# A vision tower on one core: another order in attention, slot 0's passes split around the logits, and other slots for VectorE's high parts

## The reference

```
h = tok(x); h = concat(cls, h)                         # 64 x 170 x 128
h = h + attn(layernorm(h))    # a graph convolution: relu, two adjacency products, a projection
h = h + ffn(layernorm(h)):
    hx = layernorm(x, g, b); q, k, v = hx@Wq, hx@Wk, hx@Wv       # 2 heads of 64
    q, k = l2norm(q)*sqrt(64)*qn_g, l2norm(k)*sqrt(64)*kn_g
    y = (softmax(causal(q k^T / 8)) v) @ Wo
    gate = softmax(y @ gate_W + gate_b)                # 8 experts
    hid = gelu(y @ W1[e] + b1[e])                      # 128 -> 512 for each e
    out = sum_e gate[e] * (hid @ W2[e] + b2[e])        # 512 -> 128
```

## Time and profile before

| | us |
|---|---|
| three runs | 1540.8, 1546.08, 1545.88 |
| median | 1545.88 |
| profiled execution | 1542.88 |
| its span, first to last instruction | 1540.7 |
| TensorE busy in the span | 1462.2 (95%) |
| VectorE, ScalarE, GpSimd busy | 1238.6, 1082.8, 329.9 |

### The profile page before, as it was taken

The page is one execution under the profiler, slowest core; times in us unless marked ns, Lnnn a source line. Parts: engine busy times, 40 slices in busy tenths (PEclk is TensorE's granted clock), DMA queues, the critical chain, the costliest instruction groups (busy, mean ns, idle before and its releaser), DMA issues.

```text
span 1540.7 us, 31400 instructions
## 1 busy us (share of the span) xinstructions
PE 1462.2 (95%) x10991; PEld 994.6 (65%) x10991; DVE 1238.6 (80%) x2585; ACT 1082.8 (70%) x1861; POOL 329.9 (21%) x337
## 2 busy tenths in 40 slices
PE   7898889999999999999999999999999999999998
PEld 4554556666666666666666666666666666666665
DVE  6768798878888888888888788888788888887765
ACT  5232667777777777786777777786777777777766
POOL 1135044030121313130211313130211213130101
PEclk9998899999999999999999999999999999999979
DMA  7866053333324242434233242433333242433324
GB/s 241 202 155 140 2 164 46 101 45 100 45 61 84 27 115 39 103 42 104 42 92 53 32 113 36 109 45 100 42 94 50 47 95 34 110 44 102 54 92 55
DMA packets 40340, 125.55 MB, mean 81 GB/s; under 512 B 5744, under 2 KB 5744, under 8 KB 38128
## 3 DMA queue, kind: packets, MB, share of 16 engines
q0 software_dynamic: 22464, 55.81, 25.7%
q1 hardware_dynamic: 17696, 69.28, 12.7%
q10 hardware_dynamic: 144, 0.01, 0.0%
HBM read 68.98 MB, written 50.48 MB: 78 GB/s over the span
## 4 chain that ended last, share of the span: by engine, by line
PE 59%; DVE 22%; issue 9%; ACT 7%; DMA 2%; DVEq 1%; ACTq 0%; POOLq 0%
PE pair L1009 18%; PE pair L1028 18%; PE pair L779 6%; DVE area L1434 4%; PE pair L766 4%; DVE area L1447 3%; ACT area L645 3%; PE pair L943 3%; PE pair L931 3%; DVE mx L1332 2%; ACT area L640 2%; DVE root_t L1267 2%; PE pair L807 2%; DVE area L1347 2%; PE pair L950 2%
## 5 line engine op out<-in xcount | busy, mean ns | idle before, releaser
L640 ACT ACTIVATE area<-pair,pack_b_sb 128x680 f32<-128x680 f32 x512 | 422.6, 828 | 208.1 <-PE pair L1009 206.3
L1434 DVE TENSOR_TENSOR area<-area 128x680 f16<-128x680 f32 x512 | 458.2, 898 | 128.7 <-ACT area L645 124.1
L1028 PE MATMUL pair<-area,ws 128*128 128x340 f16 x3072 | 527.9, 308 | 15.7 <-DVE area L1447 11.8
L1009 PE MATMUL pair<-area,ws 128*128 128x340 f16 x3072 | 530.2, 308 | 1.4
L1028 PEld LDWEIGHTS pair<-area,ws 128*128 128x128 f16 x3072 | 286.4, 98 | 178.9 <-DVE area L1447 44.0
L1009 PEld LDWEIGHTS pair<-area,ws 128*128 128x128 f16 x3072 | 295.3, 98 | 144.1 <-ACT area L645 3.6
L475 POOL DMA_DIRECT2D tower_out<-area x128 | 109.9, 859 | 1030.7 <-DVE area L1447 979.7
L645 ACT ACTIVATE area<-pair,pack_b_sb 128x680 f16<-128x680 f32 x384 | 316.6, 825 | 0.0
L1447 DVE SCALAR_TENSOR_TENSOR area<-pair,pack_b_sb,area 128x340 f32<-128x340 f32 x256 | 133.6, 562 | 9.4 <-PE pair L1028 9.2
L604 ACT ACTIVATE area<-pair,nbias,root 85x85 f32<-85x85 f32 (+1 forms) x256 | 112.4, 463 | 4.2 <-DVE nbias L1335 4.2
L766 PE MATMUL pair<-area,pack_a_sb 128*128 128x392 f32 (+1 forms) x260 | 92.7, 499 | 17.5 <-DVE area L1254 14.4
(11 more groups left out here) (222 smaller groups left out, 1772.8 us busy)
## 6 DMA issues: line engine op xcount, KB each, us to landing
tower_out<-area POOLq DMA_DIRECT2D x128, 340.0 KB, 4.6
area<-gate_scratch SPq DMA_DIRECT2D x16, 1360.0 KB, 10.0
area<-gate_scratch SPq DMA_DIRECT2D x16, 1020.0 KB, 7.3
area<-cells SPq DMA_DIRECT2D x16, 392.0 KB, 4.9
area<-cells POOLq DMA_DIRECT2D x14, 392.0 KB, 6.5
area<-area POOLq DMA_DIRECT2D x14, 392.0 KB, 4.3
tower_out<-ht SPq DMA_DIRECT2D x16, 340.0 KB, 2.3
area<-gate_scratch SPq DMA_DIRECT2D x16, 340.0 KB, 4.7
```

The costliest lines, as they stand in the source:

```text
L640: nc.scalar.activation(two(hid[slot % NHID]), halves(hid_ps[slot % 2]), ACT.Gelu_apprx_tanh, bias=col(COL_B1 + slot)).then_inc(hid_ready, 1)
L1009: last = mm(hid_ps[slot % 2][:, j, 0:TH], lhs[:, w], rhs[:, j * TH:(j + 1) * TH], start=(i == 0), stop=(i == 2))
L1028: last = mm(eo_ps[:, j, 0:TH], lhs[:, w], rhs[:, j * TH:(j + 1) * TH], start=(m % CH == 0 and i == 0), stop=(m % CH == CH - 1 and i == 2))
L1434: v.tensor_tensor(hl[slot % NPART], hid[slot % NHID], hh[slot % NPART], ALU.subtract).then_inc(hlo_ready, 1)
```

## The change

Four things differ.

- The slots in which VectorE makes the high part are (0, 7, 9, 11, 14, 19, 26, 28) in place of (0, 4, 8, 12, 16, 20, 24, 28). Their number stays eight. The waits that count them follow.
- In attention TensorE has graph step 2 between the transposes of images 0 and 1, graph step 3 ahead of the transposes of image 3, and the first projection ahead of the weighting of image 2. VectorE copies the first half of the values ahead of the normalisation of image 1, and the first turned probabilities ahead of the normalisation of image 2.
- TensorE's slots 0 and 1 are made by `experts_first`: the first logits, the first halves of both slots, slot 0's second half with y's high part ahead of the low part's pass, then the second logits, then slot 1's second half. In all slots the order of the three passes is high-high, low-high, high-low.
- ScalarE makes slot 0's gelu ahead of the tanh.

```diff
+DVE_HI = (0, 7, 9, 11, 14, 19, 26, 28)
@@
         def hi_on_act(slot):
-            return slot % CH > 0
+            return slot not in DVE_HI
         def his(g, slot):
-            return g * (SLOTS - E) + len([n for n in range(slot) if hi_on_act(n)])
+            return g * (SLOTS - len(DVE_HI)) + len([n for n in range(slot) if hi_on_act(n)])
@@ ScalarE
+            def gate_tanh(g):
                 act.wait_ge(lg_step, 4 * (g + 1))
                 nc.scalar.activation(lge[:, :], lg[:, :], ACT.Tanh, scale=0.5).then_inc(lge_ready, 1)
...
+                if slot == 0:
+                    gate_tanh(g)
@@ TensorE
+            def hidden_read(g, slot):
+                if hi_on_act(slot):
+                    pe.wait_ge(hhi_act, his(g, slot + 1))
+                else:
+                    pe.wait_ge(hid_ready, g * SLOTS + slot + 1)
...
                 if later:
-                    pe.wait_ge(hhi_act, his(g, 0) - 1 + m)
+                    hidden_read(g - 1, SLOTS - 2 + m)
...
                 turn_probs(g, 0)
+                graph_of(2)
                 turn_probs(g, 1)
-                graph_of(2)
                 weigh(g, 0)
                 turn_probs(g, 2)
                 weigh(g, 1)
+                graph_of(3)
                 turn_probs(g, 3)
-                graph_of(3)
+                project(g, 0)
                 weigh(g, 2)
-                project(g, 0)
                 weigh(g, 3)
                 graph_of("mean2")
                 project(g, 1)
...
+            def of_y(slot, j, parts=range(3)):
+                w = slice(slot * D, (slot + 1) * D)
+                for i in parts:
+                    lhs, rhs = ((w1h, yh), (w1l, yh), (w1h, yl))[i]
+                    last = mm(hid_ps[slot % 2][:, j, 0:TH], lhs[:, w], rhs[:, j * TH:(j + 1) * TH],
+                              start=(i == 0), stop=(i == 2))
+                return last
+            def experts_first(g):
+                pe.wait_ge(wlo_done, 1)
+                logits(g, 0)
+                of_y(0, 0)
+                of_y(1, 0)
+                pe.wait_ge(yh_ready, 2 * (g + 1))
+                of_y(0, 1, range(2))
+                pe.wait_ge(yl_ready, 2 * (g + 1))
+                of_y(0, 1, range(2, 3)).then_inc(hid_ps_ready, 1)
+                logits(g, 1)
+                of_y(1, 1).then_inc(hid_ps_ready, 1)
             def experts_in(g, slot):
-                n = g * SLOTS + slot
-                if slot >= 2 and hi_on_act(slot - 2):
-                    pe.wait_ge(hhi_act, his(g, slot - 1))
-                elif slot >= 2:
-                    pe.wait_ge(hid_ready, n - 1)
-                if slot % CH == 0:
-                    pe.wait_ge(wlo_done, 2 * (slot // CH) + 1)
-                w = slice(slot * D, (slot + 1) * D)
-                for j in range(2):
-                    if slot == 0:
-                        logits(g, j)
-                    for i, (lhs, rhs) in enumerate(((w1h, yh), (w1h, yl), (w1l, yh))):
-                        last = mm(hid_ps[slot % 2][:, j, 0:TH], lhs[:, w], rhs[:, j * TH:(j + 1) * TH],
-                                  start=(i == 0), stop=(i == 2))
-                last.then_inc(hid_ps_ready, 1)
+                if slot == 0:
+                    experts_first(g)
+                if slot >= 2:
+                    hidden_read(g, slot - 2)
+                    if slot % CH == 0:
+                        pe.wait_ge(wlo_done, 2 * (slot // CH) + 1)
+                    of_y(slot, 0)
+                    of_y(slot, 1).then_inc(hid_ps_ready, 1)
@@ VectorE
                 normalise(g, 0)
+                values_out(g, 0)
                 normalise(g, 1)
-                values_out(g, 0)
                 values_out(g, 1)
+                turned(g, 0)
                 normalise(g, 2)
-                turned(g, 0)
                 turned(g, 1)
                 normalise(g, 3)
                 turned(g, 2)
...
-                    dve.wait_ge(hhi_dve, g * E + slot // CH + 1)
+                    dve.wait_ge(hhi_dve, g * len(DVE_HI) + DVE_HI.index(slot) + 1)
```

## The result

| | before | changed | ratio, 95% interval |
|---|---|---|---|
| median of six runs each, us | 1542.12 | 1523.13 | 0.9872 [0.9849, 0.9895] |
| spread of the runs | 1540.0 to 1546.08 | 1517.99 to 1527.07 | |
| profiled execution, span | 1542.88, 1540.7 | 1517.99, 1515.8 | |

The account below looks back on a forecast made before the run. VectorE's order in the stretches TensorE waits on was taken as the bound. Gains of 1.26 us a steady group, 20.4 in all, took 1542.88 to 1522.5; adjusted halfway towards the higher run median: 1524, range 1515 to 1535.

Parts of the forecast that it names:

- Transposes: Attention: with the new order the probability transposes start earlier, a 0.17 wait appears before image 2's; gain 0.54 a group.
- Transposes 2 wait over 0.5: Attention, sign of a wrong forecast: image 2's probability transposes wait over 0.5 us for its normalisation; 0.17 was expected.
- Logits and slot 0: Around the second logits: the filled 0.88 gap returns as waits at gate's turn and first out-projection; net minus 0.14 a group.
- Casts: VectorE's moved casts: waits at the first expert's end go, gain 0.47 a group, and at the third's, gain 0.44.
- The sixth expert: Sixth expert's end: slot 24's cast goes to ScalarE and TensorE's 0.23 gap grows by 0.05 a group.
- A steady group: One repeat of four images, 85.7 us before: gains 0.40 + 0.47 + 0.44 - 0.05 = 1.26.
- the reorder is eaten: Rival: new waits at transposes 2 and gate's turn eat the reorder, casts pay (or the reverse); about 1530 to 1532; 0.12.
- nothing is left: Rival: the time saved in attention and at the experts is lost at gate's turn and sixth expert; about 1541; 0.07.
- third rival: Rival: waits of 0.9 and 0.5 near the gate lower TensorE's clock, 2.5 us a group, about 1558; slower 0.05.
- the clock leaves 1.00 in steady groups: TensorE, sign of a wrong forecast: the granted clock in steady groups falls below full, where it was 1.00 before.
- The last group: Last group: its transposes start 1.7 us earlier, but half clock follows and passes ahead of second logits cost double; counted 1.0.
- group 0: First group: transposes, waiting 4.48 us, start earlier, counted 1.4; third expert's out-projection, waiting 4.4, counted 0.3.

Follow-up runs that it names:

- attn_only: Kernel before with only TensorE's and VectorE's new attention order (plus the changed pass order in slots and form of hidden-chunk waits): 1530.09 us, ratio 0.9906.
- casts_only: Kernel before with only the new slots for VectorE's high parts (plus the changed pass order and form of hidden-chunk waits): 1531.18 us, ratio 0.9926.
- slot0_only: Kernel before with slots 0 and 1 split around the second logits and slot 0's gelu ahead of the tanh: 1547.44 us, ratio 1.0022.
- no_slot0: Changed kernel with slot 0's passes around the logits as before and the tanh first: 1512.22 us, ratio 0.9824.
- filler: Changed kernel with six more matmul passes of 340 columns, read by nobody, ahead of the gate's turn: 1513.11 us, ratio 0.982.
- tanh_first: Changed kernel with slot 0's gelu behind the tanh again, passes as changed: one run of 1523.77 us.
- slot0_on_act: Changed kernel with slot 0's high part as a second gelu on ScalarE behind the tanh, instead of VectorE's cast: 1514.08 us, ratio 0.9828.

## Why the prediction was right, and what in it was not

- **Transposes.** VectorE's order came out as stepped through: the normalisation of image 2 ends at 682.91, 72.27 behind the 610.64 of the plan, and the two groups lie 72.16 apart (the preceding graph step starts at 679.22 and 607.06). The third transposes start at 682.97, 0.06 later than planned. The new wait ahead of them is 0.39 (0.54 counted from the first set) and not 0.17, because TensorE arrives earlier: the first set of six transposes was issued in 0.45 where I had 0.52. The rest of the way to the means took 4.40 and not 4.65, and that is where the gain grew: most pieces are a little shorter than placed, the fourth transposes (0.46 for 0.55) most. Gain 0.73 (0.69 + 0.04) against 0.54. "Transposes 2 wait over 0.5" was named as a sign that the forecast is wrong; by the wider count it came, and it cost nothing of the gain.
- **Logits and slot 0.** Right in sign, size and mechanism for an undisturbed group: 0.16 lost ahead of the logits, 0.04 won behind them, 0.12 net against 0.14. The waits foreseen at the gate's turn (0.9) and at the first out-projection (0.5) measure 0.96 and 0.66. The turned gate's copy, not the subtraction alone, is the last thing there.
- **Casts.** 0.56 for 0.47 and 0.52 for 0.44: I counted the gap ahead of the first of the six passes only, and the second half of the gated sum also held up the fourth pass (0.22 idle of the weight load at 634.36 and 651.92 of the trace of before); that goes too. The sixth expert lost the 0.05 forecast.
- **A steady group** thus gains 1.64 and not 1.26, 5.7 us more over 15.
- **The other two rivals.** Neither "the reorder is eaten" nor "nothing is left" holds, since attn_only and casts_only each keep their gain. What was lost is slot 0's part alone (slot0_only, no_slot0), which the forecast had counted as a small loss.
- **The clock.** This was the third rival, at 0.05, with "the clock leaves 1.00 in steady groups" as a sign that the forecast is wrong. It does so, in some groups of some executions, and not in all of them as the rival had it: 1.0 us where it happens, 3 groups in the profiled execution. The sum put this term at nothing. What it takes from the median is put at the distance to filler, 10 us by the medians and 8 by the ratios, of which a trace shows 4.6.
- **The last group.** I counted 1.0 won. The profiles have 0.7 won in its attention (84.32 to 82.55 between the last two tanhs, 1.03 of it in the slots before) and 1.3 lost behind the last tanh (63.4 to 64.7), where the gate's turn now waits 1.82 and the clock falls; with the filler it is 63.1. Of group 0 and the prologue nothing can be said from single profiles, as they vary by more.

So the median agrees with the forecast within 1 us because errors cancel, and that closeness is luck. The kernel before was 2.3 us faster over six runs than the 1544.4 that the forecast started from (1542.12), and the terms were 5.7 too small: 1524 less these is 1516.0. The clock, which the sum did not hold, and what remains in group 0 and the last group bring it back by 7.1 to 1523.13.

The rule of the Trainium skill weighed there (TensorE: Matmul & The Clock Gate, A second HAM failure mode) describes short idles that make the clock swing. I set it aside since the gaps of 0.70 and 0.88 before left the clock at 1.00. The runs agree with it: 0.96 and 0.66, about 2 us apart, sometimes lower it, and filling the first ends that (filler), as does a return to one gap of 0.88 and one of 0.66 further apart (no_slot0: second logits at 605.76, first out-projection at 611.37).

## What to carry to other kernels

In this kernel one engine waits for a chain of another, and moving independent work into the gap brought nothing, since the chain itself did not become shorter: the passes moved ahead of the logits came back as a longer wait at the gate, and put one pass into the chain. Step through the follower's in-order queue to the next wait on the same chain before counting a filled gap as won. And look at the granted clock of each repeat, not only at its mean: two waits close together can cost more by the clock than by their own length, and a few idle passes in such a wait were worth 8 to 10 us here.

## What was not expected of the hardware

- A fall of the clock cost 0.43 to 0.50 us a group in slot0_only, 0.73 in tanh_first, 1.0 in the changed kernel and 1.3 to 1.5 in slot0_on_act, though each stretch at half clock is about as long (0.51 to 0.52 in windows of 3.4 or 3.5 us). An estimate from these: 3.4 us at half clock put TensorE 1.7 behind, and a later wait that is there anyway takes some of it back. With the 0.66 at the first out-projection that leaves 1.04 (changed kernel, measured 1.0); with that and the 0.47 at expert 0's end 0.57 (slot0_only, 0.43 to 0.50); in slot0_on_act neither wait is there. tanh_first's 0.73 is not explained by it, and none of this was tested.
- Work for nobody can pay: 6 passes a group, 0.87 us of TensorE each time, took 8 to 10 us off the median.
- Two-input VectorE steps beside GpSimd's subtraction slow down in the changed kernel too (1.35 us at 632.37 where its like takes 0.19), now 0.2 us behind the GpSimd step's start at 632.15; the cast moved to slot 11 ended before it, as forecast.
